# Six early pairs, not four, normalised within the layernorm

## The reference

```
xn = layernorm(x)                                    # each row on its own, no gamma or beta
neighbour = segment_sum(edge_weight * xn[src], dst)  # the part around the change
gnn = l2norm(leaky(xn @ W1.T + b1 + (neighbour + neighbour * xn) @ W2.T + b2))
mix = linear attention over all nodes, 8 heads, then gelu(.. @ w1) @ w2 + xn
x   = x + gnn + mix
x   = x + ffn(layernorm(x))                          # 8 experts, one per token, limited capacity
```

## Time and profile before

| | |
|---|---|
| median of 3 runs | 2567.49 us (2563.9 to 2570.61) |
| the profiled execution's own time | 2563.88 us |
| its span | 2562.1 us |
| PE busy | 2064.5 us (81%), 12911 matmuls |
| DVE busy | 1507.8 us (59%) |
| ACT busy | 1025.1 us (40%) |
| POOL busy | 1812.3 us (71%), of it the 1600 gathers of L874: 1536.6 us |
| mean granted TensorE clock | 0.913 |
| first main gather of POOL | 123.78 us |

### The profile page before, as it was taken

The page is one execution under the profiler, slowest core; times in us unless marked ns, Lnnn a source line. Parts: engine busy times, 40 slices in busy tenths (PEclk is TensorE's granted clock), DMA queues, the critical chain, the costliest instruction groups (busy, mean ns, idle before and its releaser), DMA issues. The chain is left out here.

```text
span 2562.1 us, 42813 instructions
## 1 busy us (share of the span) xinstructions
PE 2064.5 (81%) x12911; PEld 1594.8 (62%) x12911; DVE 1507.8 (59%) x5297; ACT 1025.1 (40%) x2450; POOL 1812.3 (71%) x1891
## 2 busy tenths in 40 slices
PE   0069999965677778999989998779898888876798
PEld 0035665543555557777767776557787776665787
DVE  6765555553567777876566565556566656545223
ACT  4733333311444545443443443333444443432233
POOL 7377777777777777777777777777777777722554
PEclk9979999986888889899999998889999999888999
DMA  9756666644666676777777776668888887756897
GB/s 333 271 163 170 174 174 175 171 138 143 185 189 192 201 257 215 237 240 230 238 252 223 229 248 202 218 199 267 317 295 279 308 288 254 257 197 229 316 353 259
DMA packets 279484, 594.70 MB, mean 232 GB/s; under 512 B 48486, under 2 KB 177263, under 8 KB 257008
## 3 DMA queue, kind: packets, MB, share of 16 engines
q0 software_dynamic: 93312, 256.68, 33.0%
q1 hardware_dynamic: 155553, 284.06, 32.1%
q10 hardware_dynamic: 30390, 51.21, 5.4%
HBM read 506.61 MB, written 87.99 MB: 232 GB/s over the span
## 5 line engine op out<-in xcount | busy, mean ns | idle before, releaser
L874 POOL DMA_INDIRECT rows_sb<-xn_scratch,src_sb x1600 | 1536.6, 960 | 520.9 <-issue 517.2
L1141 PE MATMUL bank<-acc 128*128 128x128 f32 (+1 forms) x2624 | 443.3, 323 | 16.8 <-issue 10.1
L962 PE MATMUL bank<-rows_sb,s_sb 128*24 128x256 f32 x3200 | 237.5, 418 | 236.7 <-DMA rows_sb<-xn_scratch,src_sb 235.7
L1141 PEld LDWEIGHTS bank<-acc 128*128 128x128 f32 x2624 | 386.2, 206 | 42.4 <-issue 21.1
L1162 PE MATMUL bank<-acc 128*128 128x256 f32 x1680 | 412.5, 389 | 0.0
L1899 ACT ACTIVATE acc<-bank,acc 128x128 f32<-128x128 f32 (+1 forms) x656 | 212.0, 398 | 384.4 <-PE bank L1141 380.6
L1162 PEld LDWEIGHTS bank<-acc 128*128 128x128 f32 x1680 | 313.9, 194 | 49.6 <-issue 0.4
L1420 DVE TENSOR_TENSOR acc<-acc,bank 128x48 f32 x832 | 170.4, 205 | 266.5 <-PE bank L972 159.4
L962 PEld LDWEIGHTS bank<-rows_sb,s_sb 128*24 128x24 f32 x3200 | 87.9, 107 | 313.0 <-issue 273.6
L1820 ACT COPY sums<-bank 120x256 f32<-120x256 f32 x208 | 76.6, 368 | 390.9 <-PE bank L962 390.4
L1851 ACT ACT_TABLE_LOAD x95 | 121.9, 1283 | 180.3 <-PE bank L1051 179.3
(11 more groups left out here) (239 smaller groups left out, 3553.9 us busy)
## 6 DMA issues: line engine op xcount, KB each, us to landing
acc<-ffn_first_in SPq DMA_DIRECT2D x82, 1028.0 KB
acc<-ffn_w_in SPq DMA_DIRECT2D x82, 1024.0 KB
rows_sb<-xn_scratch,src_sb POOLq DMA_INDIRECT x1600
arena<-xn_scratch SPq DMA_DIRECT2D x194, 128.0 KB
h_scratch<-arena ACTq DMA_DIRECT2D x97, 256.0 KB
xnt_scratch<-arena SPq DMA_DIRECT2D x97, 128.0 KB, 2.3
arena<-xnt_scratch SPq DMA_DIRECT2D x97, 128.0 KB
arena<-x_in SPq DMA_DIRECT2D x97, 128.0 KB
```

The costliest lines, as they stand in the source:

```text
L874: pool.indirect_dma_start(out=rows_sb[:, c % ROW_SLOTS, :], out_offset=None, in_=xn_d, in_offset=bass.IndirectOffsetOnAxis(ap=src_sb[:, c: ...
L962: m = pe.matmul(psum[0][i * COLS:i * COLS + WIN, 0:D], s_sb[:, p % S_SLOTS, i * GROUP + j, :], early_row(c) if p < EARLY_PAIRS else rows_s ...
L1141: m = pe.matmul(bank[:, i * tokens:(i + 1) * tokens], w1_sb[k % 2][:, h, f * P:(f + 1) * P], xt[:, k % 2, h, 0:tokens], start=h == 0, stop ...
```

## The change

Only the list `early_at` changes. Before, pairs 0 to 3 have their sums in batches 2, 5, 7 and 9 and their norms in 3, 6, 8 and 10; pairs 4 to 7 have everything in places 0 to 3. After, pairs 0 to 5 have their sums in batches 2, 4, 6, 8, 10 and 12 and their norms in 3, 5, 7, 9, 11 and 13; pairs 6 and 7 have everything in places 0 and 1. No instruction is added or taken away.

```diff
-        early_at = [2, 5, 7, 9] + [NB + e for e in range(EARLY_PAIRS - 4)]
+        early_at = [2, 4, 6, 8, 10, 12] + [NB + e for e in range(EARLY_PAIRS - 6)]
         EARLY_DONE = sum(v < NB for v in early_at)
```

## The result

The changed kernel takes 2580.35 us (median of 4 runs, 2579.39 to 2584.75) against 2565.69 (4 runs, 2563.63 to 2570.61): ratio 1.0047, 95% interval 1.0031 to 1.0063, that is 8 to 16 us, + 14.7 us by the medians. It is slower, by about half a per cent.

The account below looks back on a forecast made before the run. The layernorm's end starts POOL's row gathers, whose unbroken run sets the end. The layernorm's + 14.0 us, with the 7.2 us saved in the places booked at zero, on the median of 2567.5 gave 2581.5 us; range 2574 to 2588.

Parts of the forecast that it names:

- What sets the end: POOL's row gathers: the layernorm's end starts them, their unbroken run sets the end; first gather at 137.8, before 123.78.
- Root to root: Layernorm, between ACT's roots of successive batches: the last root comes at 130.5 and not at 116.56, + 14.0 us.
- The ten terms: Layernorm, batch 4 to batch 14: one root-to-root time per batch, from 11.92 down to 6.30, 6.74 last, sum 85.3 us.
- Count and spacing: Layernorm: the prediction gave one price for the whole change, + 14.0 us, with no split into count and spacing.
- Places: Places 2 and 3 become light: 7.2 us saved, pair 8 ends at 160.0; the saving is booked at zero.
- price of a single heavy place: PE, pairs 0 to 8: a place with a norm costs 5.8 us, one without 2.2, so 3.6 saved each.
- PE's idle time before L962: PE's wait ahead of its matmuls on gathered rows, 236.7 us before: expected up by some 7 us.
- The tail: The work behind the last unbroken gather, behind 2242 us before: follows the last rows and keeps its length.
- signs of being wrong: First gather before 132, POOL's stretch from first to last gather changed by over 3 us, or the tail's length changed.
- The idle time of the layernorm: Rival: gaps in the layernorm hide the added work; half hidden 2574.5, all 2567.5; chances 0.09 for 2574 by either way, 0.02.
- PE did not set the pace after pair 8: Rival: PE sets the pace from pair 8 on, + 6.8 us, 2574.3; chance 0.09 for 2574 by either way.
- The rule weighed: Keep the matmul engine going: lighter places 2 and 3 would end 7.2 us sooner but for the layernorm; weighed against.

Follow-up runs that it names:

- e3: Kernel before with early_at = [2, 5, 7, 9, 11, 13], six pairs in the layernorm, the first four where they were: 3056.3 us against 3048.2, ratio 1.0013.
- e11: Kernel before with early_at = [2], one pair in the layernorm and the rest in places 0 to 6: 2580.7 us against 2569.3, one run each.
- e5: The changed kernel again, no edit, against the kernel before, in the slower condition: 3063.2 us against 3043.5, ratio 1.0058.
- e12: Kernel before with 22 linked dummy ACTIVATEs ahead of the last batch's store: 3061.2 us against 3054.5, one run each.
- e4: Kernel before with 22 linked dummy ACTIVATEs ahead of the last batch's store: 3063.2 us against 3048.2, ratio 1.0045.
- e10: Kernel before with 22 linked dummy ACTIVATEs ahead of the last batch's store: 3067.6 us against 3051.4, ratio 1.0049.
- e9: Kernel before with early_at = [2, 5, 7, 9, 11, 13], the same edit as e3: 3058.2 us against 3051.4, ratio 1.0013.

## Why the prediction was right

The forecast was + 14.0 us and 2581.5; measured were + 14.7 and 2580.35 (the forecast stood on a median of 2567.5 for the kernel before, which with a fourth run is 2565.7). The interval of the times, 8 to 16 us, would not tell 14.0 from 10; what bears the mechanism out is the trace. By its own steps:

- *What sets the end.* Right: the wait ahead of the first main gather took the whole loss (14.8 of idle time), and POOL's run kept its length (+ 0.8 us, I allowed 3).
- *Root to root.* The ten terms and what they measured: 11.92 / 12.05, 8.61 / 8.62, 10.28 / 10.42, 8.61 / 8.61, 10.28 / 10.30, 7.67 / 7.66, 7.25 / 7.25, 7.67 / 7.66, 6.30 / 6.08, 6.74 / 6.65. Sum 85.33 / 85.30. Small errors cancel, which is luck: edge step 2's first operation took 1.20 us and not 1.02, batch 4 with its sums took 0.13 more than its term, and on the other side a batch of 4 tiles saves aggregates too, which I had left out. The missing 0.4 us of the first gather are the load of batch 3, which ends DVE's wait 0.5 later (root at 37.09, before 36.59); that root also differs by 0.2 between the two profiles of before.
- *Count and spacing.* The prediction priced the change as a whole, rightly. Of its 13.9 us from batch 4's root to the first gather, the count costs 8.6 with the pairs spaced as in e3; the other 5.3 are the spacing. About 1.8 of them come from the edge steps: in the changed kernel the long steps 2 and 4 stand beside sums and lengthen the chain (10.42 + 10.30 + 7.25 us), before it was steps 1, 3 and 5 (9.21 + 9.36 + 7.64), while edge step 0 sets batch 4 in both. Most of the rest is the last norm, which the changed kernel has in batch 13, ahead of the last root, and e3 in batch 14, where it delays no store.
- *Places.* Pair 8's end 160.66, forecast 160.0. The saving is 7.0 (forecast 7.2), and it is worth nothing, as booked. But the price of a single heavy place was an average over unlike ones; used beyond the four of before, where the norm is of the next pair, it failed (e11: 7.16 a place).
- *PE's idle time before L962.* Wrong: I expected 7 us more, it is 235.8 after 236.7. PE does wait for rows earlier: up to 300 us it has 8.4 us of such waits, before none. But from 300 to 2241 us they are 205.1, before 223.6, and 10.3 us in the same stretch ended with DVE's weights (L1400) instead, before 0.9. So it was given back in many places over the run; what moved it there I did not follow.
- *The tail.* I said that it keeps its length. In the profiled execution it was 5.7 us longer, at a lower granted clock. By the letter, this was one of my signs of being wrong. Against taking it as one: it differs by 2.3 us between two profiles of the kernel before, it is 324.7 in e11, and in the 3050 condition it is 339.4 for the changed kernel (e5) and 339.0, 342.5 and 347.4 for the places as before (e12, e4, e10). The medians differ by 14.7, the gathers by 14.2 to 15.2, which leaves little for the tail, though the interval of the times would allow a few us either way.
- *Rivals.* The idle time of the layernorm took nothing in. PE did not set the pace after pair 8 in the 2566 condition. It does in the 3050 condition, where the wait at the 25th gather is 15 to 42 us, and even there the change is slower. No profile of the kernel before was taken in that condition; as an estimate, e12, e4 and e10 without their 15.85 us of dummies put its 25th gather at 215.7 to 219.1, and the changed kernel's goes at 230.0, so pair 8 itself came 11 to 14 us later there.
- *The rule weighed.* Raising the use of the matmul engine where it waits (the Trainium skill, Perfetto Trace Analysis, Optimization Strategies) did not pay here: PE's stretch up to pair 8 became 7 us shorter, and then PE stood for the rows of pair 10. The Trainium skill speaks there of the engines that block the critical path; ACT and DVE in places 2 and 3 held up PE, but PE did not hold up POOL.

## What to carry to other kernels

When work is moved from behind a hand-over to before it, look for the engine whose unbroken run begins at that hand-over. What is added before it on the chain is paid once, and what is saved behind it counts only if that engine would have waited. Here the kernel before stood where both sides reach the 25th gather almost together, 153.2 against 154.0. Moving two pairs forward lost 14, since the 7 us saved in the places bought nothing. Moving three back lost some 12, since the layernorm gave back only 10 us, held by loads of x, and the places cost 23. Three and five pairs, and six in e3's spacing, were not tried in the 2566 condition, so the kernel before is the best of three, not a shown optimum.

An added wait between two engines in step can be priced from root to root to some two tenths of a microsecond, if for each batch the row of one of like make is taken. It fails where something else takes over: the loads of x in e11, or the ring that closes when the work is needed in the very next place. And where the work is put counts, not only how much of it: behind the last store it costs the hand-over nothing.

## What the runs showed of the hardware

The same kernel took 2568 us at one time and 3044 at another on the same chip (3), and in the longer condition there are gaps of 0.97 us that have no releaser between equal instructions of one engine, and DVE is busy 31.2 of the first 100 us (e5) where it was 70.9 in the first profile of the changed kernel. A conclusion from the one condition (POOL never waits for PE) does not hold in the other (it waits 201 us, in e5). Whoever compares two kernels should look first at the absolute time of the kernel before, measured beside them.

A DMA that stands behind ACTIVATEs in ACT's program need not wait for them: in e9 the last store went out 0.12 us after the first of eight norms had begun, with the other seven still to come. In e12 the same store did wait for the 22 dummies (164.25 to 180.10, issued at 180.13), each of which waits for the one before it. So a late norm and a late linked chain of the same length are not the same thing for a store behind them.
